# Codebook gathers that add in the DMA, in a fused wavelet convolution and vector quantization

## The reference, cut to what matters

```
def _L1_conv_ref(x, codebook):          # codebook: 512 x 32
    b, h, w, d = x.shape                # 8, 128, 128, 32
    xf = x.reshape(b * h * w, d)
    x_sq = jnp.sum(xf ** 2, axis=1, keepdims=True)
    c_sq = jnp.sum(codebook ** 2, axis=1)
    dists = x_sq - 2.0 * (xf @ codebook.T) + c_sq
    idx = jnp.argmin(dists, axis=1)
    return codebook[idx].reshape(b, h, w, d)

x = x + _L0_conv_ref(_gn(x), ...)       # _gn: normalization per channel
x = x + _L1_conv_ref(_gn(x), L1_conv_codebook)
return x
```

## Time and profile before

| | |
|---|---|
| median of 3 runs | 2165.28 us (2164.94 to 2166.05) |
| span of the profiled execution | 2164.4 us |
| TensorE busy (matmul) | 1984.8 us, 92% |
| VectorE busy | 1810.3 us, 84% |
| ScalarE busy | 1059.2 us, 49% |
| GpSimd busy | 1252.3 us, 58% |
| gathers, L1053 | 1024 instructions, 1000.9 us of GpSimd |
| additions, L1067 | 64 instructions, 82.5 us of GpSimd |

### The profile page before, as it was taken

One profiled execution on the slowest core, in us unless ns is written; L12 is line 12 of the kernel. 1 busy time (PEld: TensorE's weight loads), 2 busy tenths in 40 slices (PEclk: granted clock), 3 DMA queues, 4 the chain that ended last, 5 costly groups with the idle time before them and its releaser, 6 DMA issues. The chain is left out here.

```text
span 2164.4 us, 27115 instructions
## 1 busy us (share of the span) xinstructions
PE 1984.8 (92%) x5232; PEld 946.5 (44%) x5232; DVE 1810.3 (84%) x3979; ACT 1059.2 (49%) x2018; POOL 1252.3 (58%) x1299
## 2 busy tenths in 40 slices
PE   6999999999999999999999999999999999995653
PEld 3444455444544455444544445444544445442221
DVE  4122799988999799988999899988999889888996
ACT  5134645545555545546556454546455454543331
POOL 2001277654776377663776367673776457673876
PEclk9999999999999999999999999999999999995555
DMA  6000011111110112111111111111111011110111
GB/s 203 15 10 5 20 40 43 27 29 34 46 35 21 41 36 47 25 24 41 42 36 26 42 35 41 30 24 37 43 41 26 20 25 34 30 25 20 34 37 32
DMA packets 80459, 76.97 MB, mean 36 GB/s; under 512 B 29200, under 2 KB 62608, under 8 KB 80016
## 3 DMA queue, kind: packets, MB, share of 16 engines
q1 hardware_dynamic: 45776, 50.78, 8.3%
q0 software_dynamic: 32768, 16.84, 5.2%
q10 hardware_dynamic: 1728, 7.41, 0.9%
HBM read 41.36 MB, written 16.78 MB: 27 GB/s over the span
## 5 line engine op out<-in xcount | busy, mean ns | idle before, releaser
L1053 POOL DMA_INDIRECT vqc<-in_codebook,idx x1024 | 1000.9, 977 | 545.2 <-DVE idx L964 306.4
L542 PE MATMUL ring<-hf,w_sb 128*128 128x512 f32 x1824 | 888.5, 600 | 2.9 <-ACT hf L715 2.9
L487 PE MATMUL score<-cst,yst 98*128 98x512 f32 x1024 | 788.4, 777 | 83.8 <-DVE idx L964 54.8
L960 DVE MAX8 top<-score 128x8 f32<-128x512 f32 x1024 | 695.3, 684 | 74.7 <-PE score L487 63.8
L964 DVE FIND_INDEX8 idx<-top,score 128x8 uint32<-128x512 f32 x1024 | 704.2, 690 | 0.0
L666 ACT CAST yst<-bands 32x256 fp32r<-32x256 f32 x1024 | 411.3, 402 | 174.6 <-PE score L487 162.1
L542 PEld LDWEIGHTS ring<-hf,w_sb 128*128 128x128 f32 x1824 | 341.6, 191 | 316.9 <-issue 294.2
L487 PEld LDWEIGHTS score<-cst,yst 98*128 98x128 f32 x1024 | 204.0, 202 | 395.0 <-DVE idx L964 206.3
L542 PE MATMUL ring<-ha,w_sb 128*128 128x512 f32 x704 | 347.5, 598 | 5.1 <-DVE ha L853 4.6
L542 PE MATMUL ring<-hb,w_sb 128*128 128x512 f32 x544 | 262.6, 595 | 6.8 <-DVE hb L866 6.8
L627 ACT ACTIVATE z<-ring,prm 128x512 f32<-128x512 f32 x144 | 99.0, 688 | 273.3 <-PE ring L542 272.7
(11 more groups left out here) (101 smaller groups left out, 1276.8 us busy)
## 6 DMA issues: line engine op xcount, KB each, us to landing
xnat<-in_x SPq DMA_DIRECT2D x128, 128.0 KB, 2.7
yst<-yl SPq DMA_DIRECT2D x512, 32.0 KB
vqc<-in_codebook,idx POOLq DMA_INDIRECT x1024
out<-vqc SPq DMA_DIRECT2D x128, 128.0 KB
w_sb<-in_weights ACTq DMA_DIRECT2D x1, 1920.0 KB, 8.2
w_sb<-in_weights ACTq DMA_DIRECT2D x3, 384.0 KB, 12.8
w_sb<-in_weights ACTq DMA_DIRECT2D x1, 1152.0 KB, 15.6
w_sb<-in_weights ACTq DMA_DIRECT2D x1, 960.0 KB, 8.6
```

The source lines that it names most:

```text
L487: nc.tensor.matmul(score[BANK["tile", t]][:, :], yst[0:KST, j % 2, g, wp], cst[0:KST, :], start=True, stop=True).then_inc(s_tile, 1)
L542: t = nc.tensor.matmul(ring[g % RING][:, :, :], w_sb[:, SLOTS[n, m, kind, ky], :], own(source(n, m, kind), half, slice(PAD + di, PAD + di ...
L960: nc.vector.max(top8[:, t % 4, :], score[BANK["tile", t]][:, :]).then_inc(s_top, 1)
L1053: nc.gpsimd.indirect_dma_start(vqc[:, c % 2, w * CH:(w + 1) * CH], None, codebook[:, :], bass.IndirectOffsetOnAxis(idx[:, c % 2, k, 0:1], ...
```

## The change

The addition on GpSimd goes. The pixel values are copied to `ync` first, and the gather is told to add (`compute_op=ALU.add`) onto them, so `ync` holds the result and is stored; `vqc` and the semaphore `s_add` go. The waits follow: the store waits for all 16 gathers of its chunk (16 x 16 = 256 counts), the copy of pixel values for the store of chunk c - 2, the first gather of a chunk for the copy, and the first maximum of a chunk for the gathers of chunk c - 2 (for c of 0 and 1, for the last stores of the image before).

```diff
@@ -262,7 +262,6 @@
         z = sb("z", [P, 2, HALF, ROWS])
         hsum = sb("hsum", [P, JN, ROWS])
         ync = sb("ync", [P, 2, CW])
-        vqc = sb("vqc", [P, 2, CW])
         idx = sb("idx", [P, 2, 16, 8], U32)
         top8 = sb("top8", [P, 4, 8])
         st1 = sb("st1", [P, XCHUNKS, 6])
@@ -334,7 +333,6 @@
         s_yT = sem("s_yT")
         s_yev = sem("s_yev")
         s_gather = [sem(f"s_gather{i}") for i in range(2)]
-        s_add = sem("s_add")
         s_store = [sem(f"s_store{i}") for i in range(2)]
         s_yedge = sem("s_yedge")
         s_bnv = sem("s_bnv")
@@ -380,11 +378,11 @@
                                  ).then_inc(s_x[k % 2], 16)
 
             def store(v, c):
-                sp.wait_ge(s_add, PRIMED + XCHUNKS * v + c + 1)
+                sp.wait_ge(s_gather[c % 2], 256 * ((XCHUNKS // 2) * v + c // 2 + 1))
                 for e in range(2):
                     sp.dma_start(ov[v, e, :, c * CW:(c + 1) * CW] if isinstance(v, int) else
                                  ov[bass.ds(v, 1), e, :, c * CW:(c + 1) * CW].rearrange("b i n -> (b i) n"),
-                                 vqc[e * ROWS:(e + 1) * ROWS, c % 2, :]).then_inc(s_store[c % 2], 16)
+                                 ync[e * ROWS:(e + 1) * ROWS, c % 2, :]).then_inc(s_store[c % 2], 16)
 
             sp.dma_start(idn[:, :], ident[:, :]).then_inc(s_ident, 16)
             for k in range(2):
@@ -696,7 +694,7 @@
 
             def ycopy(v, c):
                 act.wait_ge(s_yT, XCHUNKS * v + c + 1)
-                act.wait_ge(s_add, PRIMED + XCHUNKS * v + max(c - 1, 0))
+                act.wait_ge(s_store[c % 2], PRIMED + 32 * ((XCHUNKS // 2) * v + c // 2))
                 dst = ync[:, c % 2, :].rearrange("p (j g w c) -> p j w g c", g=4, w=2, c=CH)
                 src = score[BANK["ychunk", c]][:, :].rearrange("p (j w g c) -> p j w g c", g=4, w=2, c=CH)
                 for j in range(2):
@@ -955,7 +953,10 @@
             def maximum(v, t):
                 if t % CTILES == 0:
                     c = t // CTILES
-                    dve.wait_ge(s_add, PRIMED + XCHUNKS * v + max(c - 1, 0))
+                    if c < 2:
+                        dve.wait_ge(s_store[c], PRIMED + 32 * (XCHUNKS // 2) * v)
+                    else:
+                        dve.wait_ge(s_gather[c % 2], 256 * ((XCHUNKS // 2) * v + c // 2))
                 wait_apart(dve, s_tile, TILES * v + t + 1, s_passed[0])
                 nc.vector.max(top8[:, t % 4, :], score[BANK["tile", t]][:, :]).then_inc(s_top, 1)
 
@@ -1047,12 +1048,12 @@
             def gather(v, t):
                 c, k = t // CTILES, t % CTILES
                 if k == 0:
-                    pool.wait_ge(s_store[c % 2], PRIMED + 32 * ((XCHUNKS // 2) * v + c // 2))
+                    pool.wait_ge(s_yev, XCHUNKS * v + c + 1)
                 wait_apart(pool, s_idx, TILES * v + t + 1, s_passed[1])
                 w = 8 * (k // JTILES) + 2 * (k % BLK) + k % JTILES // BLK
                 nc.gpsimd.indirect_dma_start(
-                    vqc[:, c % 2, w * CH:(w + 1) * CH], None, codebook[:, :],
-                    bass.IndirectOffsetOnAxis(idx[:, c % 2, k, 0:1], 0)).then_inc(s_gather[c % 2], 16)
+                    ync[:, c % 2, w * CH:(w + 1) * CH], None, codebook[:, :],
+                    bass.IndirectOffsetOnAxis(idx[:, c % 2, k, 0:1], 0), compute_op=ALU.add).then_inc(s_gather[c % 2], 16)
 
             def low(v, par, j):
                 pool.wait_ge(s_yh, JN * v + j + 1)
@@ -1060,12 +1061,6 @@
                     pool.wait_ge(s_yst[j % 2], STACKED * ((JN // 2) * v + j // 2))
                 nc.gpsimd.tensor_tensor(yl[:, j % 2], bands[par][:, :, j].rearrange("p w e i -> p w (e i)"),
                                         yh[:, j % 2], ALU.subtract).then_inc(s_yl, 1)
-
-            def add(v, c):
-                pool.wait_ge(s_yev, XCHUNKS * v + c + 1)
-                pool.wait_ge(s_gather[c % 2], 256 * ((XCHUNKS // 2) * v + c // 2 + 1))
-                nc.gpsimd.tensor_tensor(vqc[:, c % 2, :], vqc[:, c % 2, :], ync[:, c % 2, :], ALU.add)\
-                    .then_inc(s_add, 1)
 
             def attend(b, m):
 
@@ -1089,18 +1084,14 @@
                         if t % JTILES == JTILES // 2 and t // JTILES + 2 < JN:
                             low(v, 1 - par, t // JTILES + 2)
                         gather(v, t)
-                        if t % CTILES == 5 and t > CTILES:
-                            add(v, t // CTILES - 1)
                     elif nxt and what == "var1":
                         norm(0, b + 1)
                     elif conv and what == "mm":
                         for m in range(3):
                             if SPAN["wca", m, 1][1] == i:
                                 attend(b, m)
-                if quant:
-                    add(v, XCHUNKS - 1)
-
-            for counter in (s_add, *s_store):
+
+            for counter in s_store:
                 pool.sem_inc(counter, PRIMED)
             nc.gpsimd.memset(power[:, :], -0.5)
             tiles = [t for pair in (*hf, (lln,), side, ha, hb) for t in pair]
```

## The result

| | before | changed |
|---|---|---|
| median | 2165.57 us (2164.94 to 2166.05) | 2538.97 us (2536.56 to 2539.23) |
| ratio, 95% interval | | 1.1721 (1.1704 to 1.1738) |
| span of the profiled execution | 2164.4 us | 2534.7 us |

The change costs 17%: 370 us of span instead of the 8.75 us gained. The page of the changed kernel says where, if the instruction that was changed is read first. In part 5 a group is followed by busy us, mean ns of one, and the idle time before it; part 3 has packets, MB and share of the DMA engines.

What follows compares the result with a forecast made beforehand. Seven passes were taken as bound by TensorE, the last by GpSimd's chain. -8.05 (seven additions) - 1.4 (tail) + 0.7 (landing) + 0 (issue) = -8.75 us, giving about 2156.5 us; range 2153 to 2290.

Steps and rivals of the forecast that it cites:

- the issue of the gather: GpSimd's time per accumulating gather: bounded between +0 and +0.94 us over the plain 0.94, taken as +0.
- fourth case: Rival: above 0.26 us extra per gather GpSimd bounds all seven convolving, quantizing passes; 2284 us at 0.35; chance 0.23.
- The rule that spoke for it: Descriptor generation on GpSimd's DMA path is small, so the gather's issue stays near 0.94 us.
- rule on the other side: A reducing transfer emits two read descriptors a chunk, one per source; it spoke for GpSimd bounding everything.
- The case that came: GpSimd bounds every convolving, quantizing pass because gathers cost above 0.26 us more; up to about 2885 us; chance 0.23.
- the threshold of 0.074 us: Extra issue per gather at which the last pass's 127 gathers use up the 9.45 us gained.
- The landing: Tail after the last gather: reading the destination adds 0 to 1.38 us, taken as 0.7 us, paid once.
- GpSimd's chain: Last pass: GpSimd's gathers, subtractions and additions bound it; seven additions at 1.15 us give 8.05, the tail 1.4.
- The store wait: ScalarE's copy waits for the store of chunk c-2: covered by 1.1 us in the last pass; uncovered 12.6 us.
- The sign named for the fourth case: Middle passes grow, with TensorE waiting for stacks in them.
- the additions cost nothing in the middle passes: Middle passes are TensorE's, so removing GpSimd's additions there is worth nothing on TensorE's path.

Runs made afterwards that it cites:

- e2_after_plain: The changed kernel with a plain gather in place of the accumulating one (pixel values left out of the sum): 2139.82 us, ratio 0.9876.
- e3_after_four: The changed kernel with four ync chunk buffers instead of two, so the copy of chunk c waits for the store of chunk c-4: 2536.84 us, ratio 1.1708.
- f10_add_chunk: The changed kernel with plain gathers and seven additions of 128x512 on an unused buffer per pass, at the old additions' places: ratio 0.9973.
- f9_memset_chunk: The changed kernel with plain gathers and seven GpSimd memsets of 128x1064 per pass, at the old additions' places: ratio 1.0013.
- g2_after_plain: The changed kernel with plain gathers, run again on a chip where the kernel before is slower: 2313.92 us, ratio 1.0092.
- f4_memset_each: The changed kernel with plain gathers and a GpSimd memset of 128x730 after each: 2536.05 us, ratio 1.1094 to the kernel before beside it.
- r6_ladder_accum: The changed kernel with accumulating gathers of 128, 96, 64 and 32 rows, two chunks each: 2439.06 us.
- g5_memset_little: The changed kernel with plain gathers and a GpSimd memset of 128x330 after each: 2222.12 us, ratio 0.9696.

## Why the prediction was wrong

**The step that failed is the issue of the gather.** The prediction bounded it by 0 and 0.94 us, took the lower end, and the accumulating gather holds GpSimd for 0.61 us more than the plain one. The reason given, that plain gathers hold 0.94 us whatever codes they pick, says nothing about another form of the instruction, and a price of 0.44 us that doesn't depend on size can't be seen in any plain row. With x = 0.615 in the prediction's own fourth case the last pass gives 0.615 x 127 - 8.75 = +69.4 us (measured +66.1) and a middle pass 0.615 x 128 - 33 = +45.7 (measured +45.1). Seven of these make +320 where +305 were measured: the first of the seven grew by 43.2, the last, which has no next image, by 36.1. The mechanism, its place and its threshold were on record as the fourth case; the size decides, and it had no row.

The rule that spoke for it was right as far as it goes. From 32 to 128 rows a plain gather grows by 0.08 us, which agrees with what the Trainium skill says in DMA: Bandwidth & Descriptors, Anatomy of one DMA — SWDGE (gpsimd) path, that many descriptors can be emitted before the extra cost shows. It was applied to a term that is for the most part no matter of the number of rows. The Trainium skill's rule on the other side, the second read descriptor of a reducing transfer (Collectives: The Full Stack, The bandwidth ceiling), could, if its cost goes by the row, at most stand behind the part that grows with the rows, 0.17 of the 0.61 us; no run here separates reads from writes.

**The chances.** The case that came had 0.23, and the range ended at 2290, an x of about 0.35, though the upper bound of the sum itself was 0.94 with 2885 us. Between bounds whose values decide the sign in either direction, all that is below the threshold of 0.074 us is a thirteenth of the interval; nothing in the trace put the value there.

**The landing** was given 0.7 us and takes none. The last gather and the store in the timelines of GpSimd and SyncE of the changed kernel:

```profile
2528.46 1.56 POOL L1054 DMA_INDIRECT ync<-in_codebook,idx  x1 [0.30 <-issue]
...
2531.39 1.10 SPq L383 DMA_DIRECT2D out<-ync  x2
```

From the gather's end at 2530.02 to the store it is 1.37 us; before, gather to landing was 1.38.

**Right:** the last pass is GpSimd's chain and the additions stand in it (9.4 us measured for 9.45, e2_after_plain). The store wait is covered (e2_after_plain, and e3_after_four by taking it away). The sign named for the fourth case, TensorE waiting for stacks in the middle passes, is what the trace shows.

**Wrong without consequence here:** that the additions cost nothing in the middle passes. Without them, and with the new waits, a middle pass is 2.8 us shorter on the chip of the first runs. I read those passes as TensorE's because it is busy 234.9 of 241 us, but VectorE is busy for 222.3 of them, and some of its rows run longer beside GpSimd's reads. That is a possible way and is not shown. The length of a middle pass itself is 247.1 us between its marks; the 241 of the prediction were the width of the stretch that I had cut.

## What to carry to other kernels

An accumulating indirect DMA isn't the plain one with an addition for nothing: here it holds GpSimd for 0.61 us more a gather, 128 gathers an image, to save eight additions of 1.29. So one count decides before anything is built: work removed per transfer (8 x 1.29 / 128 = 0.08 us) against the extra issue per transfer. And where an operation has no row in the trace and its bounds enclose the threshold, give the chances by where the threshold lies between the bounds, or measure one such instruction first.

## What the runs showed of the hardware that was not expected

- The accumulating form of an indirect DMA has a price of its own of about 0.44 us (estimated from 0.485 at 32 rows and 0.61 at 128), and 1.3 ns more a row; it sends 144 packets for 128 rows of 128 bytes where the plain one sends 32. Why there is a fixed part stays open.
- A VectorE row with two inputs that meets a reading addition on GpSimd takes 1.82 us on average instead of 0.68 (before and f10_add_chunk, the scaled sum of 128x512); beside a memset of GpSimd it doesn't grow (f9_memset_chunk).
- GpSimd's rows overlap when an instruction follows a gather. In the changed kernel the subtraction starts at 1726.65, 0.98 us into a gather that runs from 1725.67 to 1727.23, and its row is 1.34 us long instead of 0.74. It ends at 1727.99, 0.76 us after the gather, and a subtraction between gathers adds 0.62 us to their distance, before 0.60: by these distances its own work isn't longer, its row is. Means of such rows (1303 ns against 743 here) must not be taken as a slower instruction.
- On the chips where the kernel before takes 2262 to 2288 us, ScalarE stops for 6 to 13 us while GpSimd issues gathers back to back. A case in the trace of g2_after_plain, ScalarE's and GpSimd's timelines:

```profile
1529.39 5.08 ACT L673 COPY side<-hf 32x960 f32<-32x960 f32 x5
1546.36 0.58 ACT L690 COPY xt<-score 128x512 f32<-128x512 f32 x1 [11.89 <-remote]
```

```profile
1536.84 0.94 POOL L1054 DMA_INDIRECT ync<-in_codebook,idx  x1 [0.30 <-issue]
...
1544.33 0.94 POOL L1054 DMA_INDIRECT ync<-in_codebook,idx  x1 [0.30 <-issue]
1545.58 0.94 POOL L1054 DMA_INDIRECT ync<-in_codebook,idx  x1 [0.30 <-issue]
```

  The transposes that ScalarE copies were done at 1538.5. It goes on at 1546.36, when the last gather of the row ends (1546.52), and the same coincidence within 0.6 us stands at five other places of this trace, from 733 to 1811 us; others of its long waits end 1 us or more from the end of such a row. A memset after each gather breaks the rows up and makes the kernel 92 us faster there. In the waits of the whole span this is a group of its own, which e2_after_plain, the same program on the first runs' chip, doesn't have:

```profile
ACT xt L690 <- remote: 95.3, 12, 12.6
```

  What ScalarE waited for there, no view shows; the cause stays open. The kernels in which gathers stand further apart show little of it: f4_memset_each and r6_ladder_accum, both from such chips, have no wait on "remote" at all, and g5_memset_little has 11.3 us on this line. No kernel that GpSimd bounds was run on both kinds of chip, so that such a kernel isn't touched is likely and not shown.
